# Latent attention's prologue: roots by logarithm ahead of the copies, weights of the next stage quantised inside the pair loop

## Chip, cores and metric

One core of one Trainium2 chip runs the whole kernel. The metric is the device time of one execution in microseconds (us), median over several runs.

## What is computed

The reference is a decoder of two layers over `x` with 8 rows of 128 tokens and 256 features. Each of six stages is a layer norm, an operation, and an addition to `x`: (1) a spectral attention, (2) a long convolution with the context, (3) a mixture of 8 experts of which each token takes 2, (4) latent attention, (5) cross attention with int8 weights, (6) a ternary feed-forward. The change lies in stage 4 and in the preparation of stage 5:

```python
def _layernorm(x, axis=-1, eps=1e-05):
    m = jnp.mean(x, axis=axis, keepdims=True)
    v = jnp.var(x, axis=axis, keepdims=True)
    return (x - m) / jnp.sqrt(v + eps)
...
q_latent = hidden_states @ Wqa
q = (q_latent @ Wqb).reshape(b, s, H, Q_HEAD_DIM)
kv_comp = hidden_states @ Wkva
c_kv, k_pe = (kv_comp[..., :KV_LORA], kv_comp[..., KV_LORA:])
q_pe, k_pe = _apply_rope(q_pe, cos, sin), _apply_rope(k_pe, cos, sin)
scores = jnp.einsum('bhqd,bhkd->bhqk', q_full, k_full) * scale   # 16 heads, causal
probs = jax.nn.softmax(scores, axis=-1)
out = (probs @ v) @ Wo
...
def _qdq(x):                       # stage 5, weights and activations
    s = jnp.maximum(jnp.max(jnp.abs(x), axis=-1, keepdims=True) / 127.0, 1e-08)
    return jnp.clip(jnp.round(x / s), -127.0, 127.0) * s
```

## The kernel before

Every engine has its own instruction stream, written out by hand in one block each (`sp`, `pool`, `act`, `dve`, `pe`), and the streams meet only at semaphores: `wait_ge` holds everything that stands behind it on its engine. Nothing is scheduled by a planner; the order of the source is the order on the engine. `then` on VectorE (DVE) chains an instruction to the one before it.

Stage 3 ends with 16 gathers on GpSimd (POOL, L489): four per pair of token rows, semaphore `gathered{pair}`. SyncE (SP) issues, from L411 on, the weights of stage 5 (`w5_loaded`) and the transposed context (`cxT_loaded`) as soon as the last expert product is in PSUM (`l3_psum`).

Stage 4 works on four pairs of rows. Its prologue, before the pair loop, does for each pair i: `add_experts(i)` on DVE (the expert rows are added to `x`, L1110, with the statistics, L889), then `normalise(4, ...)` (L899): variance plus eps into `ve` (`ln_var`), a root, `rsqrt_refined` (one Newton step), and `xn` (L909). The root is taken on ScalarE (ACT) by `deviation(n, lo, hi)` (L550): `sd = sqrt(ve)`, and DVE takes the reciprocal of it (L881). TensorE (PE) turns `xn` (`turn_pair(i)`, L1579), ACT copies it out of PSUM (`xnT_pair(i)`). For pair 0 alone the prologue also has PE make the latents (`latents`), eight groups of queries (`queries_low`, `queries_high`, L1623 and L1627, in two alternating PSUM banks) and the keys (`key_latents`, `turn_kv`); ACT copies each group (`queries(0, j)`, L704), POOL rotates it (`rope_q`, L499 to L503), and PE may start group j only when ACT has copied group j - 2 (`q4_copied`). Behind the last pair, DVE quantises the stage-5 weights `ew` (L1170 to L1178: largest value, scales, `ediag`, `eqf`, `eqi`), and only then gives the semaphores `s4_masked`, `pT_ready`, `x4_added` their start values.

`pair4(i, after)` is then the attention of pair i, with the queries of pair i + 1 worked in: a `Fori` of three rounds on each of PE, ACT, DVE and POOL, and a fourth call without a next pair. Its waits count with the loop register. Per round POOL rotates eight query groups and divides eight groups of probabilities (`divide`, L508). The tail of a round is the products with the values, the output projection (L1682), `rope_k(after, u)` (L1147 to L1152) and `add_tile` (L1120) on DVE.

`preload(f)` on ACT (L548) is an activation on one value whose only use is that the table of `f` is loaded then: `Sqrt` ahead of the prologue, `Exp` ahead of the pair loop, `Sqrt` behind it, `Exp` and `Sqrt` around stage 5's pair loop.

## Time and profile before

| | us |
|---|---|
| three runs | 782.61, 782.74, 784.62 (median 782.74) |
| the profiled execution | 780.92 |
| its span, first to last instruction | 778.7 |
| PE, DVE, ACT, POOL busy | 587.9, 462.9, 309.4, 261.6 |
| granted TensorE clock, mean | 0.885 of full |

The profile covers one execution, whose time is 2.2 us more than its span. All times below are microseconds from the span's start. A busy share over the whole span mixes six stages with different limits. What the change is worth has to be read in the stretch from 374, where stage 3 ends, to 437, where the first round of the pair loop has POOL busy, and at the two roots of stages 5 and 6 (near 608 and 709).

### The profile page before, as it was taken

What the parts mean: (1) busy time and instruction counts of PE and PEld (TensorE: products, weight loads), DVE (VectorE), ACT (ScalarE), POOL (GpSimd) and SP (SyncE); (2) the same over time, 40 slices, a digit from 0 to 9 for tenths busy, and PEclk for the clock granted to TensorE, in tenths of its full rate; (3) what the DMA queues carried; (4) which work ended last, traced back from release to release, by engine and by line L of the source; (5) the groups of instructions that cost most, each with busy time, mean ns of one, the idle gap of its engine ahead of it and who ended that gap; (6) DMA issues with size and microseconds to landing.
All of it is one profiled execution on the core that took longest, in us unless ns stands there. A gap on an engine that the chain in (4) does not pass through costs nothing.

```text
span 778.7 us, 12968 instructions
## 1 busy us (share of the span) xinstructions
PE 587.9 (75%) x4241; PEld 425.7 (55%) x4242; DVE 462.9 (59%) x1004; ACT 309.4 (40%) x738; POOL 261.6 (34%) x300
## 2 busy tenths in 40 slices
PE   3857896455599999999174989989888677762665
PEld 3446343334488888898032656656576265552333
DVE  3677999674455455554168352524445846868695
ACT  1511201425233333333122562736555445554463
POOL 4930688758000000000466580936713310100000
PEclk9979999556699999999776899999999999996697
DMA  7693202456311111110610000000000400000000
GB/s 271 226 388 127 86 1 70 147 182 243 109 36 45 54 54 38 43 55 29 196 49 0 0 1 1 0 0 0 0 0 1 162 1 2 2 2 1 0 27 28
DMA packets 34245, 52.11 MB, mean 67 GB/s; under 512 B 3096, under 2 KB 24160, under 8 KB 33824
## 3 DMA queue, kind: packets, MB, share of 16 engines
q1 hardware_dynamic: 31680, 43.49, 16.7%
q0 software_dynamic: 2528, 8.13, 2.8%
q8 instruction: 23, 0.38, 0.2%
q14 instruction: 14, 0.11, 0.0%
HBM read 40.60 MB, written 11.01 MB: 66 GB/s over the span
## 4 chain that ended last, share of the span: by engine, by line
PE 45%; DVE 19%; POOL 13%; issue 12%; ACT 7%; DMA 3%; SPq 0%; POOLq 0%; ACTq 0%; DVEq 0%
PE bank L1533 15%; PE bank L1546 5%; POOL rq L501 3%; POOL sm L508 3%; POOL sorted_rows L483 3%; POOL rq L499 2%; PE bank L1412 2%; PE bank L1682 2%; PE bank L1441 2%; DVE xn L909 2%; PE bank L1443 2%; PE bank L1442 2%; PE bank L1944 1%; ACT pT L803 1%; PE bank L1843 1%
## 5 line engine op out<-in xcount | busy, mean ns | idle before, releaser
L1533 PE MATMUL bank<-h,wsp 128*128 128x256 f16 x720 | 81.3, 273 | 2.0 <-DVE h L1088 1.2
L654 ACT ACTIVATE hf<-bank,be 128x256 f32<-128x256 f32 x120 | 50.4, 471 | 81.5 <-PE bank L1533 72.9
L489 POOL DMA_INDIRECT yg<-expert_rows,pos x16 | 15.7, 981 | 186.5 <-DMA expert_rows<-yb 181.9
L1533 PEld LDWEIGHTS bank<-h,wsp 128*128 x720 | 69.5, 98 | 12.1 <-issue 3.8
L1086 DVE CAST h<-hf 128x512 f16<-128x512 f32 x60 | 25.6, 427 | 65.5 <-ACT hf L654 64.0
L698 ACT ACTIVATE sm<-sm,nm 128x128 f32<-128x128 f32 x128 | 49.8, 394 | 1.0 <-DVE nm L1198 1.0
L471 POOL TENSOR_TENSOR kvp<-xnT,cxT 128x512 f32<-128x512 f32 x32 | 35.6, 1136 | 42.9 <-ACT xnT L558 33.0
L564 ACT CAST wsp<-wraw 128x2048 f16<-128x2048 f32 x12 | 22.6, 1900 | 66.1 <-DMA wraw<-in_L_ffn_W 66.1
L448 POOL TENSOR_TENSOR wsp<-wraw,wsp 128x512 f16<-128x512 f32 x40 | 45.8, 1176 | 8.5 <-ACT wsp L564 8.2
L1195 DVE SCALAR_TENSOR_TENSOR sm<-bank,const 128x512 f32<-128x512 f32 x32 | 22.1, 692 | 38.1 <-PE bank L1649 38.1
L1533 PE MATMUL bank<-xgT,wsp 128*128 128x256 f16 x360 | 43.9, 281 | 0.1
L499 POOL TENSOR_TENSOR rq<-qs,const 128x256 f32<-128x256 f32 x32 | 23.6, 737 | 59.1 <-ACT qs L704 59.1
L1546 PE MATMUL bank<-wsp,h 128*128 x360 | 41.9, 273 | 1.6 <-DVE h L1088 1.6
L1088 DVE TENSOR_TENSOR h<-hf,h 128x512 f16<-128x512 f32 x60 | 41.5, 692 | 2.1
L508 POOL TENSOR_TENSOR sm<-sm,rinv 128x512 f32<-128x512 f32 x32 | 33.1, 1040 | 26.1 <-DVE rinv L1189 26.1
L1533 PEld LDWEIGHTS bank<-xgT,wsp 128*128 x360 | 36.3, 101 | 5.6 <-issue 0.5
L1546 PEld LDWEIGHTS bank<-wsp,h 128*128 128x128 f16 x360 | 35.1, 98 | 5.9 <-issue 1.8
L1627 PE MATMUL bank<-wqb,ql 128*128 128x512 f32 x64 | 35.3, 639 | 0.0
L1649 PE MATMUL bank<-kT,qT 128*128 128x128 f32 x256 | 34.0, 276 | 0.9 <-ACT qT L711 0.9
L1218 DVE COPY pT<-bank 128x512 f32<-128x512 f32 x32 | 21.7, 682 | 18.5 <-PE bank L1660 18.0
L1660 PE MATMUL bank<-const,sm 128*128 128x128 f32 x128 | 22.0, 300 | 13.7 <-POOL sm L508 10.5
L1649 PEld LDWEIGHTS bank<-kT,qT 128*128 128x128 f32 x256 | 31.3, 192 | 1.5 <-ACT qT L711 1.3
(291 smaller groups left out, 1359.8 us busy)
## 6 DMA issues: line engine op xcount, KB each, us to landing
wraw<-in_L_ffn_W SPq DMA_DIRECT2D x16, 512.0 KB, 4.5
wraw<-in_L_ffn_W SPq DMA_DIRECT2D x8, 1024.0 KB
sorted_rows<-early POOLq DMA_DIRECT2D x2, 1920.0 KB, 14.3
xg<-sorted_rows SPq DMA_DIRECT2D x15, 256.0 KB, 2.8
expert_rows<-yb SPq DMA_DIRECT2D x15, 256.0 KB, 2.2
cxT<-in_ctxT SPq DMA_DIRECT2D x2, 1024.0 KB, 9.3
tap<-in_taps SPq DMA_DIRECT2D x1, 2048.0 KB, 14.3
x<-in_x SPq DMA_DIRECT2D x1, 1024.0 KB, 5.8
```

The source lines that it names most:

```text
L448: last = nc.gpsimd.tensor_tensor(wsp[:, e, 1, part], wraw[:, half, 512 * q:512 * q + 512], wsp[:, e, 0, part], ALU.subtract)
L471: nc.gpsimd.tensor_tensor(kvp[:, h % 2, c, :].rearrange("p (b i j) -> p b i j", b=NT, i=CH), xnT[:, c, :, g].unsqueeze(3).to_broadcast([P, ...
L499: nc.gpsimd.tensor_tensor(rq[:, g % 2, 0], v, cosb, ALU.mult).then_inc(sem("rope_step"), 1)
L508: nc.gpsimd.tensor_tensor(sm[:, u, hs, :], sm[:, u, hs, :], rinv[:, u, hs].unsqueeze(2).to_broadcast([P, 4, P]), ALU.mult).then_inc(sem("p ...
L654: last = nc.scalar.activation(hf[:, p, SLOTS * k:SLOTS * k + SLOTS], bank[2 * (layer - 1) + p][:, SLOTS * k:SLOTS * k + SLOTS], ACT.Gelu, ...
L698: last = nc.scalar.activation(sm[:, u, h, :], sm[:, u, h, :], ACT.Exp, bias=nm[:, u, h:h + 1], accum_out=rsum[:, u, h:h + 1])
L1086: nc.vector.tensor_copy(hi, hf[:, p, :]).then_inc(sem("h_hi"), 1)
L1088: nc.vector.tensor_tensor(h[:, 1, 2 * p:2 * p + 2, :].rearrange("p f n -> p (f n)"), hf[:, p, :], hi, ALU.subtract).then_inc(sem(f"h{layer ...
L1533: last = nc.tensor.matmul(b[:, SLOTS * (f % 2):SLOTS * (f % 2) + SLOTS], w[a_][:, c, P * f:P * f + P], inp[:, b_, c, :], start=(c == 0 and ...
L1546: last = nc.tensor.matmul(bank[4 + u][:, D * b:D * b + D], h2[:, b_, c, P * b:P * b + P], w[a_][:, c, :], start=(c == 0 and a_ + b_ == 0), ...
L1627: nc.tensor.matmul(four_heads(bank[1 + k][:]), ql0[:, u, :], wqb[:, k, :, a_:a_ + 4, :].rearrange("p w h n -> p h w n"), start=False, stop ...
L1649: last = nc.tensor.matmul(bank[5 + g % 2][:, P * k:P * k + P], qT[:, u, 4 * g + k, :], kT[:, u, :], start=True, stop=True)
```

## The change

In words, engine by engine:

- SP waits, ahead of the stage-5 loads, for the last of the gathers.
- `deviation(n, ...)` with n of 4 or more (the four of the prologue, and those of stages 5 and 6) writes ln(ve) into `sd`, waits for itself, and writes exp(-0.5 sd) into `rs`; DVE no longer takes the reciprocal. All `preload(ACT.Exp)` and `preload(ACT.Sqrt)` from the prologue on are gone, and the first is `preload(ACT.Ln)`.
- On ACT and PE the roots and the turns of pairs 1 to 3 stand further ahead between the copies and products of the queries. On DVE `rope_k(0, 0)` and `rope_k(0, 1)` stand behind the norms of pairs 2 and 3.
- The quantisation of `ew` is cut in three parts, and part i stands in the tail of pair i, ahead of its `rope_k`. The semaphores get their start values ahead of the prologue.
- The pair loop is written out on all four engines.

```diff
             sp.wait_ge(sem("l3_psum"), ET)
+            sp.wait_ge(sem(f"gathered{NT // 2 - 1}"), 16 * 4)
...
                 act.wait_ge(sem("ln_var"), n)
-                nc.scalar.activation(sd[:, lo:hi], ve[:, lo:hi], ACT.Sqrt).then_inc(sem("ln_sd"), 1)
+                if n < 4:
+                    nc.scalar.activation(sd[:, lo:hi], ve[:, lo:hi], ACT.Sqrt).then_inc(sem("ln_sd"), 1)
+                else:
+                    nc.scalar.activation(sd[:, lo:hi], ve[:, lo:hi], ACT.Ln).then_inc(sem("ln_log"), 1)
+                    act.wait_ge(sem("ln_log"), n - 3)
+                    nc.scalar.activation(rs[:].rearrange("p t k -> p k t")[:, 0, lo:hi], sd[:, lo:hi], ACT.Exp, scale=-0.5).then_inc(sem("ln_sd"), 1)
...
-            preload(ACT.Sqrt)
+            preload(ACT.Ln)
...
             deviation(4, 0, 2)
             xnT_pair(0)
+            deviation(5, 2, 4)
...
             query_latents(0)
+            xnT_pair(1)
             queries(0, 0)
             key_latents(0, 0)
-            deviation(5, 2, 4)
-            for j in range(1, 4):
-                queries(0, j)
-            xnT_pair(1)
+            deviation(6, 4, 6)
+            queries(0, 1)
+            queries(0, 2)
+            xnT_pair(2)
+            deviation(7, 6, 8)
+            queries(0, 3)
             queries(0, 4)
             key_latents(0, 1)
-            deviation(6, 4, 6)
             queries(0, 5)
-            xnT_pair(2)
-            deviation(7, 6, 8)
+            xnT_pair(3)
             queries(0, 6)
             queries(0, 7)
-            xnT_pair(3)
-            preload(ACT.Exp)
-            with act.Fori(0, NT // 2 - 1) as i:
-                pair4(i, i + 1)
-            pair4(NT // 2 - 1, None)
-
-            preload(ACT.Sqrt)
+            for i in range(NT // 2):
+                pair4(i, i + 1 if i + 1 < NT // 2 else None)
+
             deviation(8)
...
             magnitudes(0)
-            preload(ACT.Exp)
...
-            preload(ACT.Sqrt)
             outputs5(NT - 1)
...
-                then(nc.vector.reciprocal(r[:, 0], root))
+                if root is not None:
+                    then(nc.vector.reciprocal(r[:, 0], root))
...
-            for i in range(2):
-                add_experts(i)
-                normalise(4, 4 + i, 2 * i, 2 * i + 2)
-            rope_k(0, 0)
-            add_experts(2)
-            normalise(4, 6, 4, 6)
-            rope_k(0, 1)
-            add_experts(3)
-            normalise(4, 7, 6, 8)
...
             dve.sem_inc(sem("s4_masked"), 2)
             dve.sem_inc(sem("pT_ready"), 2)
             dve.sem_inc(sem("x4_added"), 1)
+            for i in range(NT // 2):
+                add_experts(i)
+                normalise(4, 4 + i, 2 * i, 2 * i + 2)
+                if i >= 2:
+                    rope_k(0, i - 2)
...
                     for t in range(NT - 2):
                         stats(5, t)
+                quantise_weights(i)
                 for u in range(2):
                     if after is not None:
                         rope_k(after, u)
...
             latents(0)
+            turn_pair(1)
             queries_low(0, 0)
...
             queries_high(0, 2)
+            turn_pair(2)
             queries_high(0, 3)
-            turn_pair(1)
             queries_low(0, 4)
             queries_high(0, 4)
             pe.wait_ge(sem("kvr_ready"), 1)
             key_latents(0, 1)
             queries_high(0, 5)
-            turn_pair(2)
+            turn_pair(3)
             turn_kv(0, 1)
             queries_low(0, 6)
             queries_high(0, 6)
             queries_high(0, 7)
-            turn_pair(3)
             pe.wait_ge(sem("xnT_act"), 10)
-            with pe.Fori(0, NT // 2 - 1) as i:
-                pair4(i, i + 1)
-            pair4(NT // 2 - 1, None)
+            for i in range(NT // 2):
+                pair4(i, i + 1 if i + 1 < NT // 2 else None)
```

The order on ScalarE before, from the root of pair 0 on (`sd` is the root, `xnT` the turned pair, `ql` the query latents, `qs` a query group, `kvT` the key latents; the names in brackets are semaphores):

```order
L553 ACTIVATE sd<-ve 128x2 [waits ln_var]
L679 COPY xnT<-bank 128x2x256 [waits xnT_psum]
L688 COPY ql<-bank 128x256 [waits lat_psum]
L689 COPY ql<-bank 128x256
L704 COPY qs<-bank 128x512 [waits q4_psum]
L693 COPY kvT<-bank 128x128 [waits kv_psum]
L553 ACTIVATE sd<-ve 128x2 [waits ln_var]
L704 COPY qs<-bank 128x512 [waits q4_psum] x3
L679 COPY xnT<-bank 128x2x256 [waits xnT_psum]
```

The same place in the changed kernel (`rs` is the inverse root; its line numbers are some lines higher):

```order
L556 ACTIVATE sd<-ve 128x2 [waits ln_var]
L558 ACT_TABLE_LOAD
L558 ACTIVATE rs<-sd 128x2 [waits ln_log]
L684 COPY xnT<-bank 128x2x256 [waits xnT_psum]
L556 ACT_TABLE_LOAD
L556 ACTIVATE sd<-ve 128x2 [waits ln_var]
L558 ACT_TABLE_LOAD
L558 ACTIVATE rs<-sd 128x2 [waits ln_log]
L694 COPY ql<-bank 128x256 [waits lat_psum]
L695 COPY ql<-bank 128x256
L684 COPY xnT<-bank 128x2x256 [waits xnT_psum]
L710 COPY qs<-bank 128x512 [waits q4_psum]
```

The root of pair 1 moved from behind the first query group to ahead of the latents, and every root is now a logarithm and an exponential with a table load ahead of each.

Further on, ScalarE before, from the second query group of pair 0 to the last root:

```order
L704 COPY qs<-bank 128x512 [waits q4_psum] x3
L679 COPY xnT<-bank 128x2x256 [waits xnT_psum]
L704 COPY qs<-bank 128x512 [waits q4_psum]
L693 COPY kvT<-bank 128x128 [waits kv_psum]
L553 ACTIVATE sd<-ve 128x2 [waits ln_var]
L704 COPY qs<-bank 128x512 [waits q4_psum]
L679 COPY xnT<-bank 128x2x256 [waits xnT_psum]
L553 ACTIVATE sd<-ve 128x2 [waits ln_var]
```

And in the changed kernel, from the root of pair 2 on:

```order
L556 ACTIVATE sd<-ve 128x2 [waits ln_var]
L558 ACT_TABLE_LOAD
L558 ACTIVATE rs<-sd 128x2 [waits ln_log]
L710 COPY qs<-bank 128x512 [waits q4_psum] x2
L684 COPY xnT<-bank 128x2x256 [waits xnT_psum]
L556 ACT_TABLE_LOAD
L556 ACTIVATE sd<-ve 128x2 [waits ln_var]
L558 ACT_TABLE_LOAD
L558 ACTIVATE rs<-sd 128x2 [waits ln_log]
L710 COPY qs<-bank 128x512 [waits q4_psum] x2
L699 COPY kvT<-bank 128x128 [waits kv_psum]
```

The last root, which waits for the variance of pair 3, moved from behind six query groups to behind three.

VectorE before, at the end of the prologue (`esc` scales, `ediag`, `eqf`, `eqi` the quantised weights; `sm` the scores of the first round):

```order
L909 TENSOR_SCALAR xn<-x,mv,rs 128x256
L1171 TENSOR_REDUCE esc<-ew 128x4 [waits w5_loaded]
L1166 TENSOR_SCALAR esc<-esc 128x4 [waits dve_own]
L1167 RECIPROCAL esc<-esc 128x4 [waits dve_own]
L1176 TENSOR_SCALAR eqf<-ew,esc 128x256 [waits dve_own] x2
L1175 TENSOR_SCALAR ediag<-const,esc 128x128 [waits dve_own]
L1176 TENSOR_SCALAR eqf<-ew,esc 128x256 [waits dve_own]
L1175 TENSOR_SCALAR ediag<-const,esc 128x128 [waits dve_own]
L1176 TENSOR_SCALAR eqf<-ew,esc 128x256 [waits dve_own]
```

VectorE in the changed kernel, in the tail of the first round (`pT` turned probabilities, `kvr` and `rk` the keys of the next pair, `x` with `bank` the added output):

```order
L1222 COPY pT<-bank 128x512 [waits pt4_psum]
L1192 RECIPROCAL rinv<-rsum 128x4 [waits exp_ready] x2
L1222 COPY pT<-bank 128x512 [waits pt4_psum] x3
L1175 TENSOR_REDUCE esc<-ew 128x4 [waits w5_loaded]
L1167 TENSOR_SCALAR esc<-esc 128x4 [waits dve_own]
L1168 RECIPROCAL esc<-esc 128x4 [waits dve_own]
L1149 COPY kvr<-bank 128x64 [waits kvn_psum,dve_own]
L1150 TENSOR_TENSOR rk<-bank,const 128x64
L1152 TENSOR_TENSOR rk<-bank,const 128x32 x2
L1154 TENSOR_TENSOR kvr<-rk 128x64 [waits rk_step]
L1122 TENSOR_TENSOR x<-x,bank 128x256 [waits out4_psum]
```

The first part of the quantisation moved out of the stretch between the last norm and the first round, to between the last copy of probabilities and the key rotation of a round's tail.

## Rows read from the trace of the kernel before

**Rows 1.** The page: busy time, share of the span, instructions of an engine.

```profile
PE 587.9 (75%) x4241; PEld 425.7 (55%) x4242; DVE 462.9 (59%) x1004; ACT 309.4 (40%) x738; POOL 261.6 (34%) x300
```

**Rows 2.** The chain that ended last, 374 to 440: start, duration, what.

```profile
380.70 6.68 DMA yg<-expert_rows,pos
...
424.78 12.68 issue
```

**Rows 3.** The gathered tile `yg`: issue to landing.

```profile
DMA to landing us min/median/max: 2.7/3.0/7.4
```

**Rows 4.** VectorE in order of time, 374 to 440: start, duration, instruction, idle before.

```profile
387.40 1.01 DVE L1110 SCALAR_TENSOR_TENSOR x<-yg,top,x 128x256 f32<-128x256 f32 x2 [16.16 <-DMA yg<-expert_rows,pos]
...
390.49 0.17 DVE L904 TENSOR_SCALAR ve<-mv 128x2 f32<-128x2 f32 x1
...
391.13 0.16 DVE L882 TENSOR_TENSOR nw<-rs 128x2 f32<-128x2 f32 x1
...
402.34 0.17 DVE L881 RECIPROCAL rs<-sd 128x2 f32<-128x2 f32 x1 [6.37 <-ACT sd L553]
...
406.33 1.34 DVE L1110 SCALAR_TENSOR_TENSOR x<-yg,top,x 128x256 f32<-128x256 f32 x2
...
409.90 0.49 DVE L904 TENSOR_SCALAR ve<-mv 128x2 f32<-128x2 f32 x1
...
422.99 1.21 DVE L1171 TENSOR_REDUCE esc<-ew 128x4 f32<-128x1024 f32 x1
...
424.87 1.07 DVE L1176 TENSOR_SCALAR eqf<-ew,esc 128x256 f32<-128x256 f32 x2
...
427.39 0.69 DVE L1177 TENSOR_SCALAR eqf<-eqf 128x1024 f32<-128x1024 f32 x1
```

**Rows 5.** Source lines of table loads and roots: shortest, median, longest, in ns.

```profile
L548 ACT ACT_TABLE_LOAD  x7: 1283/1283/1283, 196.0 to 715.0; - x7
...
L553 ACT ACTIVATE sd<-ve x9: 203/208/217, 10.1 to 709.3; 128x8 f32<-128x8 f32 x5, 128x2 f32<-128x2 f32 x4
```

**Rows 6.** TensorE in order of time, 374 to 440, and 462 to 496.

```profile
394.71 3.78 PE L1592 MATMUL bank<-xnT,wqa 128*128 128x256 f32 x8 [0.68 <-ACT xnT L679]
...
407.11 1.13 PE L1623 MATMUL bank<-wqb,ql 64*128 64x512 f32 x4 [0.24 <-ACT qs L704]
...
409.58 1.02 PE L1627 MATMUL bank<-wqb,ql 128*128 128x512 f32 x2
...
414.98 2.08 PE L1623 MATMUL bank<-wqb,ql 64*128 64x512 f32 x4
...
428.41 1.09 PE L1641 MATMUL bank<-const,qs 128*128 128x128 f32 x4 [4.17 <-DVEq L1180]
...
477.36 0.60 PE L1641 MATMUL bank<-const,qs 128*128 128x128 f32 x4
```

**Rows 7.** A stretch: busy time of PE, PEld, DVE, ACT, POOL; granted clock, DMA share, GB/s.

```profile
413.00:419.00 6.00, 5.27 (x12) 2.40 (x13) 4.41 (x12) 0.59 (x1) 4.83 (x8) 0.50 0.00 0
```

**Rows 8.** GpSimd in order of time: its first rotation of rounds 0 and 1.

```profile
437.49 0.73 POOL L499 TENSOR_TENSOR rq<-qs,const 128x256 f32<-128x256 f32 x1 [12.09 <-ACT qs L704]
...
484.70 0.73 POOL L499 TENSOR_TENSOR rq<-qs,const 128x256 f32<-128x256 f32 x1 [19.72 <-ACT qs L704]
```

**Rows 9.** VectorE in the tail of round 0.

```profile
467.50 0.21 DVE L1147 COPY kvr<-bank 128x64 f32<-128x64 f32 x1
...
470.82 0.42 DVE L1120 TENSOR_TENSOR x<-x,bank 128x256 f32 x1 [2.51 <-PE bank L1682]
```

**Rows 10.** VectorE and ScalarE at the roots of stages 5 and 6.

```profile
608.43 0.20 DVE L881 RECIPROCAL rs<-sd 128x8 f32<-128x8 f32 x1 [0.28 <-ACT sd L553]
...
709.43 3.74 ACT L832 COPY fguT<-bank 128x1024 bf16<-128x1024 bf16 x4
...
717.81 1.23 DVE L1236 TENSOR_SCALAR xn<-xn 128x2048 f32<-128x2048 f32 x1 [0.22 <-ACT xn L839]
```

**Rows 11.** DMA queues, 605 to 700: packets, MB, share of 16 engines.

```profile
q8 instruction: 8, 0.13, 0.6%
```

More of the change, by code:

```diff
@@ L523, in _ @@
                 rope_q(0, j // 4, j % 4)
-            with pool.Fori(0, NT // 2 - 1) as i:
-                pair4(i, i + 1)
-            pair4(NT // 2 - 1, None)
+            for i in range(NT // 2):
+                pair4(i, i + 1 if i + 1 < NT // 2 else None)
             pool.wait_ge(sem("x4_added"), NT + 1)
@@ L906, in normalise @@
                 r2 = rs[:].rearrange("p t k -> p k t")
-                rsqrt_refined(ve[:, lo:hi], sd[:, lo:hi], r2[:, :, lo:hi], nw[:, :, lo:hi])
+                rsqrt_refined(ve[:, lo:hi], sd[:, lo:hi] if n < 4 else None, r2[:, :, lo:hi], nw[:, :, lo:hi])
                 for t in range(lo, hi):
@@ L1152, in rope_k @@
                 nc.vector.tensor_tensor(kvr[:, u, 64:128], rk[:, 0], rk[:, 1], ALU.add).then_inc(sem("kvr_ready"), 1)
-            for i in range(2):
+            dve.sem_inc(sem("s4_masked"), 2)
+            dve.sem_inc(sem("pT_ready"), 2)
+            dve.sem_inc(sem("x4_added"), 1)
+            for i in range(NT // 2):
                 add_experts(i)
                 normalise(4, 4 + i, 2 * i, 2 * i + 2)
-            rope_k(0, 0)
-            add_experts(2)
-            normalise(4, 6, 4, 6)
-            rope_k(0, 1)
-            add_experts(3)
-            normalise(4, 7, 6, 8)
+                if i >= 2:
+                    rope_k(0, i - 2)
             def scales(dst_scale, dst_inverse, largest, floor):
@@ L1167, in scales, with quantise_weights @@
                 then(nc.vector.reciprocal(dst_inverse, dst_scale))
-            dve.wait_ge(sem("w5_loaded"), 112)
-            ew4 = ew[:].rearrange("p w c n -> p (w c) n")
-            then(nc.vector.tensor_reduce(esc[:, 0, :], ew4, AX.X, ALU.max, apply_absolute_value=True))
-            scales(esc[:, 1, :], esc[:, 2, :], esc[:, 0, :], True)
-            for k in range(4):
-                if k >= DC:
-                    then(nc.vector.tensor_scalar(ediag[:, k - DC, :], cst["ident"], esc[:, 1, k:k + 1], None, ALU.mult))
-                then(nc.vector.tensor_scalar(eqf[:, k, :], ew4[:, k, :], esc[:, 2, k:k + 1], ROUND, ALU.mult, ALU.add))
-            then(nc.vector.tensor_scalar(eqf[:], eqf[:], -ROUND, 127.0, ALU.add, ALU.min))
-            nc.vector.tensor_scalar(eqi[:], eqf[:], -127.0, None, ALU.max).then_inc(sem("eqi_ready"), 1)
-            dve.sem_inc(sem("s4_masked"), 2)
-            dve.sem_inc(sem("pT_ready"), 2)
-            dve.sem_inc(sem("x4_added"), 1)
+            def quantise_weights(part):
+                ew4 = ew[:].rearrange("p w c n -> p (w c) n")
+                if part == 0:
+                    dve.wait_ge(sem("w5_loaded"), 112)
+                    then(nc.vector.tensor_reduce(esc[:, 0, :], ew4, AX.X, ALU.max, apply_absolute_value=True))
+                    scales(esc[:, 1, :], esc[:, 2, :], esc[:, 0, :], True)
+                elif part == 1:
+                    for k in range(4):
+                        if k >= DC:
+                            then(nc.vector.tensor_scalar(ediag[:, k - DC, :], cst["ident"], esc[:, 1, k:k + 1], None, ALU.mult))
+                        then(nc.vector.tensor_scalar(eqf[:, k, :], ew4[:, k, :], esc[:, 2, k:k + 1], ROUND, ALU.mult, ALU.add))
+                elif part == 2:
+                    then(nc.vector.tensor_scalar(eqf[:], eqf[:], -ROUND, 127.0, ALU.add, ALU.min))
+                    nc.vector.tensor_scalar(eqi[:], eqf[:], -127.0, None, ALU.max).then_inc(sem("eqi_ready"), 1)
             causal = cst["causal"].unsqueeze(1).to_broadcast([P, 4, P])
@@ L1218, in copy_pT @@
                 nc.vector.tensor_copy(pT[:, u, 4 * g:4 * g + 4, :].rearrange("p h n -> p (h n)"), bank[3 + g % 2][:]).then_inc(sem("pT_ready"), 1)
-            with dve.Fori(0, NT // 2 - 1) as i:
-                pair4(i, i + 1)
-            pair4(NT // 2 - 1, None)
+            for i in range(NT // 2):
+                pair4(i, i + 1 if i + 1 < NT // 2 else None)
             nc.vector.tensor_tensor(bkm[:], bk5[:].unsqueeze(2).to_broadcast([P, DC, 2]), cst["parity"].unsqueeze(1).to_broadcast([P, DC, 2]), ALU.mult).then_inc(sem("bkm_ready"), 1)
@@ L1750, in _ @@
             queries_high(0, 7)
-            turn_pair(3)
             pe.wait_ge(sem("xnT_act"), 10)
-            with pe.Fori(0, NT // 2 - 1) as i:
-                pair4(i, i + 1)
-            pair4(NT // 2 - 1, None)
+            for i in range(NT // 2):
+                pair4(i, i + 1 if i + 1 < NT // 2 else None)
             x_done(pe, 4, NT - 1)
```

## Prediction

> **What bounds the kernel now.** I read the page first, then the chain that ended last, then each engine in order of time in the stretch that the change touches. The page says little here: TensorE is busy for 75% of the span [rows 1], but that is an average over six stages. The chain of 374 to 440 says more. The reader is to see two things in it: 6.68 us of waiting for a gather at its head, and 12.68 us from 424.78 on, in which no work of the chain runs before the pair loop has GpSimd going [rows 2]. From there a round is set by GpSimd and the tail behind it: its first rotation starts at 437.49 in round 0 and at 484.70 in round 1, 47.2 us apart [rows 8]. So all that the prologue gains shifts the time of that first rotation, and I ask when it starts after the change.
>
> The prologue before has three stalls. VectorE gets its first rows at 387.40 [rows 4], although a gather lands in 3.0 us as a rule and this one took 6.68 [rows 2, 3]: the stage-5 weights were in the queues. It then waits 6.37 us for the root of pair 1, because that root stands behind a query group on ScalarE [rows 4]. And it quantises weights from 422.99 on, while TensorE waits 4.17 us for the start values behind that work, to 428.41 [rows 4, 6].
>
> **The change, step by step** (new times on the clock of the trace before).
>
> *Gathers first.* The fourth gather is issued at 380.70; with 3.0 us it lands at 383.7, 3.7 earlier. Between 2.7 and the old 6.68 us the gain is 4.0 to 0; the first is near, since the cause of the long one is moved away. The loads behind it are needed one whole round later and stay hidden; if they came late, quantising would hold the tail of round 0.
>
> *Roots by logarithm.* A root cost 0.21 us of ScalarE and a reciprocal. It is now Ln 0.21, a table load 1.28 and Exp 0.21 in a row, since the order shows a load ahead of each of the two; the load ahead of Ln can run while the variance is awaited [rows 5]. From the variance's end at 390.66 to the Newton step at 391.13 it was 0.47 us [rows 4]; it becomes 1.75: +1.28 for each root on the path.
>
> *The chain on VectorE.* A pair's additions and statistics take 3.26 us (387.40 to 390.66) or, beside GpSimd's rotations, 4.06 (406.33 to 410.39) [rows 4]. Newton step and norm take 1.7 us for a pair, to 2.9 beside GpSimd, read from 391.13 and 402.34 on to the next additions, at most 3.1 and 4.0 with the key rotation in them. So: additions from 383.7, variance 0 at 386.9, its root at 388.7, norm 390.4. Pair 1: variance 393.6, root 395.3 (it was 402.34), norm 397.0. Pair 2: variance 400.3.
>
> *ScalarE and TensorE beside it.* TensorE turns pair 0 at 390.4 and has the latents (3.78 us) at 396.0 [rows 6]. Now it must turn pair 1 first, at 397.0 to 398, and the first query group is copied near 400.3, about 1.2 earlier than before. ScalarE copies it and the keys, and at 400.9 turns to root 2: load 1.28, Ln 0.21, load 1.28, Exp 0.21, together 3.0 us, to 403.9. Only then does it copy group 1, and TensorE can start group 2 at 404.5; here the change is some 1.1 us **behind** the kernel before. VectorE has norm 2 at 406.6, the keys at 407.5, and pair 3's variance at 411.4.
>
> *The new wait.* On ScalarE root 3 stands ahead of the copy of group 3. Its Ln waits for the variance at 411.4, and load and Exp take it to 413.1. Behind it stand the copies of groups 3 to 7, and TensorE waits for group 3's copy before group 4: it starts that at 413.7, where it was 407.11 [rows 6]. So ordering the roots ahead gives VectorE back its 6.37 us and takes 6.6 from the queries. But all four norms are then done at about 416, and nothing but query work is left.
>
> *To the first round.* From group 4 to the end of group 5 TensorE needed 3.49 us (407.11 to 410.60) at the full clock [rows 6]. The turns of pair 3 and of the keys, a wait for a copy, and groups 6 and 7, which take what 4 and 5 take, add 3.7: 7.2 in all. But TensorE has stood for some 5 us before 413.7. Before the change the clock was at 0.50, its lower level of 1.2 GHz, from 413 to 419, after TensorE had stood from 410.60, although it was busy 5.27 of those 6 us [rows 7]; the same two products took 2.08 instead of 1.13 us [rows 6]. I add 2.3 us for some 5 us at the lower clock: round 0 begins at 423.2 instead of 428.41, **-5.2**. In exchange the round begins with the clock up. From a round's first product to GpSimd's first rotation it was 9.08 us in round 0 (428.41 to 437.49) and 7.34 in round 1 (477.36 to 484.70) [rows 6, 8]: **-1.7**. First rotation at 430.5: **-6.9**. With the full clock throughout it is -9.3 (413.7 + 7.2 + 7.34 = 428.2); with the lower clock all through, 413.7 + 13 + 9.1 = 435.8, -1.7.
>
> *Quantising in the tails.* Part 0 takes 1.88 us (422.99 to 424.87), part 1 2.52 (to 427.39), part 2 1.4 [rows 4]. The room: in the tail of round 0 VectorE has its copies done at 467.5, rotates keys for 0.8 us, and then waits 2.51 us for the output product, to 470.82 [rows 9]. Parts 0 and 2 fit; part 1 ends its keys at 467.5 + 2.5 + 0.8 = 470.8: **+0.1**. Were there no room, it would be 5.8 in three tails.
>
> *Written-out loop.* The first product of round 1 follows at 477.36 with no idle time noted ahead of it [rows 6], so the way back cost nothing there: **0**. What it can cost is below.
>
> *Stages 5 and 6.* The Exp table that the removed preloads brought is there from root 8 on; both preloads stood in waits of ScalarE and give nothing. Root 8 is on the path: VectorE waits only for it at 608.43 [rows 10], so it pays 1.28 more: **+1.3**. After root 9 ScalarE copies six blocks from 709.43 on, and VectorE at 717.81 waits for ScalarE by 0.22 [rows 10]; ScalarE is later by a load and an Exp, 1.28 + 0.21: **+1.5**.
>
> Sum: -6.9 + 0.1 + 1.3 + 1.5 = **-4.0 us**. The profiled execution took 780.92, 1.8 below the median of 782.74; from the median, 778.7.
>
> **A rule against the rows.** The trace shows table loads of 1.283 us and no gap that it charges to them [rows 5], and the order shows Ln and Exp each with its own load. The Trainium skill (ScalarE: Activation LUTs, "What ACT_TABLE_LOAD costs") gives the same 1283 ns, but adds a drain of about 1380 ns to each switch of sets; by its figure each of the places above would cost twice as much, and the result would be near no change. The same page ("Table sets: the hidden batching unit") has one set that holds both Ln and Exp, with one load for the pair. The built program doesn't use it, by the order's rows.
>
> **Rivals.**
> - *A switch costs twice its load.* Four places on the path (roots 0, 3, 8, 9) would each cost another load's time, if the engine had to empty around it: 4 x 1.28 = 5.1, and 782.74 - 4.0 + 5.1 = 783.8, no change. Against it: the root in rows 10 is answered within 0.28 us, and nothing idle is charged to loads. 8%.
> - *The clock stays low through the prologue*, since TensorE now has two rests (near 402 and 409): -1.7 + 2.9 is +1.2, 783.9; half way from the forecast, 781.3. For it: rows 7; against it: the long busy run from 413.7. 12%, within 0.3% mostly.
> - *Slower: code.* Three more copies of a round on four engines must be fetched. If each new page stalled TensorE for a transfer of some 2.7 us [rows 3] in the tails, where TensorE is the path, five stalls are +13.5: 792. From two stalls (5.4) on it eats the gain, and three give 786.8. Against it: 8 such fetches lie in 605 to 700, in straight code [rows 11]. 9%.
> - *More is won.* The clock stays up (-9.3), or the loop's register work was on the path: 776.3. 14%. The Trainium skill (Runtime: NRT & Kernel Launch, "Instruction fetch mechanics") holds that a taken branch outside the fetched pages stalls; by it writing out gains, but the trace shows no stall at 477.36.
> - *The loads are not there* (one table for both): roots 0, 3, 8, 9 without 1.28, 773.6. The order speaks against it. 2%.
> - *My forecast*, 776.8 to 780.8: 55%.
>
> **Numbers.** A measurement of this kernel tells about 0.3%, 2.35 us, from no change. Faster by that is below 780.4: nearly all of the forecast's 55, the 14 and 2, in all 0.69. Within: 0.20. Slower: 0.11. The range, 775.0 to 782.8, leaves out the code rival, the full drain and the shared table, and holds the bounds of the clock in part.
>
> **What the next profile would show.** First additions on VectorE near 383.7; its wait for root 1 at 1.7 us, not 6.4; 16 table loads instead of 9; ScalarE idle ahead of the Ln of root 3, and a TensorE gap of some 5 us ending near 413.7; first round near 423; first rotation near 430.5, each round then 47.2; Newton steps of stages 5 and 6 later by 1.3 against what is ahead of them. The prediction fails if ScalarE's root 3 is released much earlier or later than 413, if the clock doesn't return before the first round, or if the rounds' period changes.

## The result, and the profile after

The changed kernel takes 776.86 us (median of four runs, 776.02 to 778.14), the kernel before in the same comparison 783.19: ratio 0.9921, 95% interval 0.990 to 0.9942. A second series gave 772.87 against 782.41, 0.9897 (0.986 to 0.9934). So it is faster by 6 to 10 us. The forecast, 778.7, had the sign and the mechanism; the gain of 4.0 was too small.

From the page of the profiled execution, which took 776.70 us where that of before took 780.92 (the row that answers to [rows 1] is the second):

```profile
span 774.9 us, 12670 instructions
PE 590.2 (76%) x4241; PEld 425.4 (55%) x4242; DVE 459.4 (59%) x998; ACT 319.3 (41%) x747; POOL 257.2 (33%) x300
```

ScalarE has 9.9 us more to do and the kernel is faster. What the busy time buys is in the order. The first gather is issued at 379.13, against 376.89 before: stages 1 to 3, which the change leaves alone, took 2.2 us longer in this execution. All times of after below carry these 2.24 us against the clock of before.

The gathered tile, and VectorE in order of time:

```profile
DMA to landing us min/median/max: 2.7/2.7/2.8
```

```profile
385.69 1.00 DVE L1112 SCALAR_TENSOR_TENSOR x<-yg,top,x 128x256 f32<-128x256 f32 x2 [12.10 <-DMA yg<-expert_rows,pos]
...
395.35 0.17 DVE L906 TENSOR_SCALAR ve<-mv 128x2 f32<-128x2 f32 x1
...
397.31 0.16 DVE L884 TENSOR_TENSOR nw<-rs 128x2 f32<-128x2 f32 x1 [1.78 <-issue]
...
401.91 0.17 DVE L906 TENSOR_SCALAR ve<-mv 128x2 f32<-128x2 f32 x1
...
405.66 0.16 DVE L884 TENSOR_TENSOR nw<-rs 128x2 f32<-128x2 f32 x1 [3.58 <-ACT rs L558]
...
412.75 0.17 DVE L906 TENSOR_SCALAR ve<-mv 128x2 f32<-128x2 f32 x1
```

The long landing of [rows 3] is gone, and the wait for the root of pair 1 fell from 6.37 [rows 4] to 1.78. What replaced it is on ScalarE, around the roots of pairs 2 and 3:

```profile
402.62 1.28 ACT L556 ACT_TABLE_LOAD   x1
403.91 0.20 ACT L556 ACTIVATE sd<-ve 128x2 f32<-128x2 f32 x1
404.13 1.28 ACT L558 ACT_TABLE_LOAD   x1
405.43 0.20 ACT L558 ACTIVATE rs<-sd 128x2 f32<-128x2 f32 x1
405.54 0.57 ACT L710 COPY qs<-bank 128x512 f32<-128x512 f32 x1
...
412.95 0.20 ACT L556 ACTIVATE sd<-ve 128x2 f32<-128x2 f32 x1 [2.19 <-DVE ve L906]
413.17 1.28 ACT L558 ACT_TABLE_LOAD   x1
414.47 0.20 ACT L558 ACTIVATE rs<-sd 128x2 f32<-128x2 f32 x1
414.58 0.57 ACT L710 COPY qs<-bank 128x512 f32<-128x512 f32 x1
```

A root for two values a lane now holds ScalarE for 2.9 us (402.62 to 405.54), and the next copy of queries starts 1.63 us after the variance of pair 3 releases ScalarE (412.95 to 414.58). TensorE, and then GpSimd:

```profile
406.16 1.13 PE L1626 MATMUL bank<-wqb,ql 64*128 64x512 f32 x4 [3.00 <-ACT qs L710]
...
415.20 2.08 PE L1626 MATMUL bank<-wqb,ql 64*128 64x512 f32 x4 [5.56 <-ACT qs L710]
...
423.90 0.60 PE L1644 MATMUL bank<-const,qs 128*128 128x128 f32 x4
```

```profile
431.21 0.73 POOL L500 TENSOR_TENSOR rq<-qs,const 128x256 f32<-128x256 f32 x1 [1.69 <-ACT qs L710]
...
476.78 0.73 POOL L500 TENSOR_TENSOR rq<-qs,const 128x256 f32<-128x256 f32 x1 [18.05 <-ACT qs L710]
```

Two new waits, 3.00 and 5.56 us, and no wait at the first round any more (4.17 in [rows 6]). The clock in the same stretch (columns as in [rows 7]):

```profile
415.00:418.00 3.00, 2.80 (x5) 1.00 (x6) 1.98 (x5) 0.14 (x1) 2.44 (x4) 0.50 0.03 5
418.00:421.00 3.00, 2.90 (x13) 1.58 (x11) 0.07 (x1) 1.37 (x4) 1.26 (x3) 0.89 0.00 0
421.00:424.00 3.00, 2.98 (x9) 1.21 (x10) 1.26 (x5) 1.05 (x2) 2.84 (x6) 1.00 0.00 0
```

After the rest of 5.56 us TensorE works at 0.50, its level of 1.2 GHz, and is back at full by the third row, before the first round. At the roots of stages 5 and 6, where [rows 10] is before, VectorE shows:

```profile
601.76 0.17 DVE L884 TENSOR_TENSOR nw<-rs 128x8 f32<-128x8 f32 x1 [1.80 <-ACT rs L558]
```

```profile
707.16 0.17 DVE L884 TENSOR_TENSOR nw<-rs 128x8 f32<-128x8 f32 x1 [1.80 <-ACT rs L558]
...
715.41 1.23 DVE L1239 TENSOR_SCALAR xn<-xn 128x2048 f32<-128x2048 f32 x1 [0.46 <-ACT xn L840]
```

### The profile page after: what moved, and what is told of

The parts are those of the page before. It is cut to its first block, busy times and chain, and to the rows that moved or that the text cites. A ratio compares the mean times of both kernels' runs of the same rounds, so it can differ in the third digit from the quotient of the medians.

```text
span 774.9 us, 12670 instructions
## 1 busy us (share of the span) xinstructions
PE 590.2 (76%) x4241; PEld 425.4 (55%) x4242; DVE 459.4 (59%) x998; ACT 319.3 (41%) x747; POOL 257.2 (33%) x300
## 4 chain that ended last, share of the span: by engine, by line
PE 52%; DVE 16%; POOL 12%; ACT 11%; issue 4%; DMA 3%; another core or an unknown queue 0%; SPq 0%; ACTq 0%; DVEq 0%
PE bank L1536 16%; PE bank L1549 5%; PE bank L1685 4%; POOL sm L509 3%; POOL rq L502 3%; POOL qs L504 2%; POOL rq L500 2%; PE bank L1415 2%; ACT pT L805 2%; PE bank L1444 2%; PE bank L1446 2%; PE bank L1445 2%; DMA wraw<-in_L_ffn_W 1%; PE bank L1845 1%; PE bank L1946 1%
## 5 line engine op out<-in xcount | busy, mean ns | idle before, releaser
L1685 PE MATMUL bank<-wo4a,oT 128*128 128x256 f32 x128 | 32.5, 404 | 0.0
L502 POOL TENSOR_TENSOR rq<-qs,const 128x128 f32<-128x128 f32 x64 | 31.9, 520 | 0.0
```

The costliest lines, as they stand in the source:

```text
L502: nc.gpsimd.tensor_tensor(turned[:, :, :, two], pairs[:, :, :, 1 - two], sinb[:, :, :, two], ALU.mult).then_inc(sem("rope_step"), 1)
L1685: last = nc.tensor.matmul(bank[7][:, 0:D], oT[:, u, j, :], wvo[:, j, :], start=(j == 0), stop=(j == H4 // 2 - 1))
```

## Experiments

To compare profiled executions I cut each into stretches between marks that every variant has. The columns: from the first gather to the first product of round 0; from there to GpSimd's first rotation; round 0 from rotation to rotation; from GpSimd's memset of stage 5 to the first Newton product of its root; from there to the variance of stage 6; from that to the first clip of VectorE (L1236 before). Values are differences of two starts, in us; the last two columns are the timed runs. The runs were taken in several series, and each ratio is to the kernel before as timed in the same series (its medians were 781.6 to 783.6), so ratios and not medians are compared across rows. A trace is of one execution: in e_wait_alone, e_start_alone, e_rolled, e_sqrt, e_shared and after_again of the shortest one timed, in e_order3 of one of the longer ones.

| kernel | to round 0 | to rotation | round 0 | root 5 | stage 5 | root 6 | median | ratio |
|---|---|---|---|---|---|---|---|---|
| before | 51.52 | 9.08 | 47.21 | 4.05 | 100.44 | 8.70 | 783.19 | 1 |
| after | 44.77 | 7.31 | 45.57 | 5.33 | 103.43 | 10.22 | 776.86 | 0.9921 |
| after_again | 44.69 | 7.30 | 45.54 | 5.33 | 101.68 | 10.22 | 772.87 | 0.9897 |
| e_wait_alone | 49.24 | 8.57 | 48.65 | 4.04 | 100.77 | 8.70 | 778.73 | 0.9956 |
| e_no_wait | 51.42 | 7.30 | 45.53 | 5.33 | 101.30 | 10.22 | 782.02 | 0.9987 |
| e_start_alone | 48.19 | 8.98 | 47.17 | 4.06 | 100.07 | 8.70 | 779.76 | 0.9972 |
| e_quant_prologue | 46.90 | 7.31 | 45.55 | 5.33 | 103.42 | 10.22 | 778.28 | 0.9938 |
| e_rolled | 44.62 | 7.40 | 45.70 | 5.34 | 104.65 | 10.22 | 778.32 | 0.9968 |
| e_sqrt | 40.20 | 8.78 | 47.22 | 4.05 | 100.90 | 8.70 | 768.84 | 0.9831 |
| e_shared | 39.15 | 7.30 | 45.57 | 4.05 | 103.39 | 8.94 | 774.73 | 0.9898 |
| shared_again | 42.29 | 7.31 | 46.99 | 4.05 | 104.67 | 8.94 | 772.95 | 0.9866 |
| e_order3 | 45.58 | 7.31 | 46.77 | 5.33 | 103.30 | 10.22 | 776.18 | 0.9934 |
| e_order3_sqrt | 35.42 | 7.95 | 47.03 | 4.05 | 100.86 | 8.70 | 765.17 | 0.9806 |
| e_order3_shared | 35.56 | 7.31 | 47.10 | 4.05 | 101.72 | 8.95 | 760.57 | 0.9728 |

The ratios' 95% intervals reach 0.002 to 0.004 to either side. Only e_order3_shared is beyond 2% with its whole interval.

**The gathers' wait, alone and taken out.** On the kernel before:

```diff
             sp.wait_ge(sem("l3_psum"), ET)
+            sp.wait_ge(sem(f"gathered{NT // 2 - 1}"), 16 * 4)
```

> The kernel before with one line of the change: SyncE waits for the last gather ahead of the stage-5 loads. My account: the first additions start 3.7 to 4.0 us earlier and everything behind them in the prologue shifts: 779.3 us, 3.9 less than before. Rival, the roots behind the query copies take it back: 783.

And the same line taken out of the changed kernel:

> The changed kernel without the wait for the last gather. My account: the first additions are 3.7 to 4.0 us later, the whole prologue with them: 780.7 us. Rival, root 3 stands on ScalarE and is bound by the table loads, not by the first gather: 777.

Alone the wait gives 0.44% (interval of the ratio 0.9931 to 0.9981), some 3.4 us. Without it the changed kernel is no faster than before: 782.02, ratio 0.9987 (0.9963 to 1.0011). Its gathers then land, in the view of the tile and on VectorE:

```profile
388.66 1.01 DVE L1111 SCALAR_TENSOR_TENSOR x<-yg,top,x 128x256 f32<-128x256 f32 x2 [17.85 <-DMA yg<-expert_rows,pos]
```

```profile
DMA to landing us min/median/max: 2.7/4.1/8.4
```

The wait for the first rows, 12.10 us in the changed kernel, is 17.85 here: the line is worth 5.75 us of VectorE's start in this execution, where the fourth gather of before landed 3.7 later than the usual 3.0. Taken out of the change it costs 0.66 to 0.90% by the two ratios of the changed kernel, the largest effect of a part tried, and without it the rest is within 0.3%. That the rest is worth nothing doesn't follow: in this trace the first additions come 12.19 us after the first gather's issue, 1.7 later than before (10.51), and TensorE has the low clock at group 0 (2.08 us for its first products), both of which are in its 51.42 us to round 0.

**The start values alone.** On the kernel before, the three increments of VectorE moved ahead of the prologue:

```diff
+            dve.sem_inc(sem("s4_masked"), 2)
+            dve.sem_inc(sem("pT_ready"), 2)
+            dve.sem_inc(sem("x4_added"), 1)
             for i in range(2):
                 add_experts(i)
...
-            dve.sem_inc(sem("s4_masked"), 2)
-            dve.sem_inc(sem("pT_ready"), 2)
-            dve.sem_inc(sem("x4_added"), 1)
```

> The kernel before with one edit: the three start values (s4_masked, pT_ready, x4_added) are given ahead of the prologue instead of behind the quantisation. My theory: the wait of 4.17 us of TensorE at the first round's start goes, so round 0 begins some 3.5 us earlier than 428.41 on the clock of before. But VectorE is still quantising until about 428, and masks and sums of the first round stand behind that, so the first rotation on GpSimd comes earlier by less: I expect 0 to 3 us, 781 to 783 where the kernel before has 783. Rival: the start values alone carry the prologue's gain, then 8 us are won and this is 775.

779.76, ratio 0.9972 (0.9951 to 0.9993), and round 0 begins 3.3 us earlier, as expected. My bound on what that is worth was too careful. VectorE in that kernel:

```profile
426.25 0.69 DVE L1181 TENSOR_SCALAR eqi<-eqf 128x1024 bf16<-128x1024 f32 x1
429.54 0.69 DVE L1195 SCALAR_TENSOR_TENSOR sm<-bank,const 128x512 f32<-128x512 f32 x1 [2.59 <-PE bank L1649]
```

Quantising ends at 426.94 and VectorE then waits 2.59 us for the first scores. The time to rotation is unchanged (8.98), so the 3.3 us reach the first rotation in full. The timed runs have 0.28% of it, some 2.2 us, with an interval from 0.5 to 3.8.

**Quantising in one piece behind the prologue,** in the changed kernel, with the start values left early:

```diff
+            for part in range(3):
+                quantise_weights(part)
...
-                quantise_weights(i)
```

> The changed kernel with the whole quantisation back in one piece, but behind the last key rotation of the prologue, with the start values given early as changed. My account: what gained was that the start values no longer stand behind it, and VectorE has about 6 us free there (from 422.3 to the first scores at 428.4) for its 5.8 us: nothing lost, 777 us. Rival, it must be in parts in the tails: 780 or more.

778.28 (0.9938, interval 0.9909 to 0.9968), within the spread of the changed kernel. The rotation comes 7.31 us after round 0 begins, as in it, and the next stretches agree to 0.05. That round 0 begins 2.1 us later in its trace is for the most part the clock, well ahead of the quantising. Group 0 of the queries, in it and in the changed kernel:

```profile
399.51 2.08 PE L1628 MATMUL bank<-wqb,ql 64*128 64x512 f32 x4
```

```profile
399.56 1.13 PE L1626 MATMUL bank<-wqb,ql 64*128 64x512 f32 x4
```

With the two products behind them (1.93 us and 1.12) that is 1.8 us. So the early start values do the work; cutting the quantisation in three gives nothing that these rows show.

**The loop rolled again** on TensorE, ScalarE and GpSimd (VectorE's stays written out):

> The changed kernel with the pair loop a loop again on TensorE, ScalarE and GpSimd (VectorE's stays written out, since the parts of the quantisation differ by round). My account: the written-out loop gives nothing, rounds are 45.5 to 47.3 us apart in either form, by the clock: 777 us, within noise of the changed kernel. Rival, the 1.6 us that round 0 lost came from writing it out: rounds of 47.2 each and 780.

Round 0 takes 45.70 and round 1 47.22, against 45.57 and 47.09. In 425 to 590, most of the four rounds, the changed kernel has more instruction fetches than the kernel before. The DMA queues, after first, then before:

```profile
q8 instruction: 7, 0.11, 0.3%
```

```profile
q8 instruction: 2, 0.03, 0.1%
```

Neither the branches of the one nor the fetches of the other are on the path in these rows. (The Trainium skill, Runtime: NRT & Kernel Launch, "Instruction fetch mechanics", warns of a stall at a taken branch outside the fetched pages; no such stall is in these rounds.) The medians, 0.9968 against 0.9921 and 0.9897, leave 3.7 to 5.6 us, and its trace, of the shortest execution, has nothing of it in the rounds. The twelve executions fall into two groups: six of 775.6 to 777.0 with a mean clock of 0.885 to 0.889, and six of 779.7 to 782.2 with 0.877 to 0.881. The upper clocks give the times of the changed kernel in the first series (776.0 to 777.0 at 0.885 to 0.887), so what differs is how many executions had the lower one, here half, there one of four (778.1 at 0.880). Whether the loop has a part in that isn't shown.

**Square roots in the new order.** The changed kernel with `Sqrt`, the reciprocal and the preloads of before:

```diff
...
-                    nc.scalar.activation(sd[:, lo:hi], ve[:, lo:hi], ACT.Ln).then_inc(sem("ln_log"), 1)
-                    act.wait_ge(sem("ln_log"), n - 3)
-                    nc.scalar.activation(rs[:].rearrange("p t k -> p k t")[:, 0, lo:hi], sd[:, lo:hi], ACT.Exp, scale=-0.5).then_inc(sem("ln_sd"), 1)
+                    nc.scalar.activation(sd[:, lo:hi], ve[:, lo:hi], ACT.Sqrt).then_inc(sem("ln_sd"), 1)
...
```

> The changed kernel with the roots of before (square root, reciprocal on VectorE, and the preloads of Sqrt and Exp put back), all else as changed: the new order alone, without the logarithm. My account: a root costs 0.47 us again, so nearly the same as with the shared set, but the Exp preload (1.5 us) stands between the last query copy and the first round: 767 us. If the logarithm itself is what gained, this gives the gain back, 780 or more.

768.84, ratio 0.9831 (0.9797 to 0.9864): the logarithm costs the change 0.66 to 0.90%, 5 to 7 us. In the stretches: 4.6 us to round 0, 1.28 at the root of stage 5, 1.52 at that of stage 6, less 1.5 to the first rotation, where the preload of `Exp` returns (417.35). The traces differ in two more stretches, round 0 (1.65 us longer) and stage 5 (2.5 shorter), for which these roots give no cause. TensorE ahead of group 4 still waits:

```profile
406.90 2.08 PE L1625 MATMUL bank<-wqb,ql 64*128 64x512 f32 x4 [4.08 <-ACT qs L705]
```

By these rows 4.08 of the 5.56 us belong to root 3's place ahead of the copy, and 1.5 to the load and the exponential.

**The set that holds both functions.** One line:

```diff
-            preload(ACT.Ln)
+            nc.scalar.preload_act_table_set("natural_log_exp_and_others")
```

> The changed kernel with one table set that holds logarithm and exponential loaded once at 680 in place of the Ln preload: 5 table loads in all instead of 16, the arithmetic the same functions. My account (each load that stands in a root is waited for, and ScalarE's loads are what holds the query copies): every Newton step follows its variance by 0.5 us instead of 1.95, root 2 is ready 3 us earlier beside that, group 4 of the queries starts some 7 us earlier, TensorE's gap and low clock ahead of it go: about -8 in the prologue and -2.6 at the roots of stages 5 and 6, 766 us. Rival, only the four loads on the old path count: -5.1, 772. Rival, a switch also drains the engine, which the records don't show: a further -1.3 for each of the switches taken away, 761 or less. Rival, the loads are hidden: 777.

> The changed kernel with the shared table set once more, for the open question why one execution took 766.6 and the other six 772.7 to 777.7. If those six had lost time to the granted clock of that stretch of executions, most executions should now lie at 765 to 768 with a mean clock of 0.89, a ratio of 0.978 to 0.983. If the variant itself has a second course, 772 to 777 comes again, ratio near 0.99, and the loads' worth in this order is then 0 to 3 us and not 8.

The loads between logarithm and exponential go, the Newton step follows the variance by 0.5 us, and roots 5 and 6 lose 1.28 us each. The step of stage 5 in e_shared:

```profile
589.04 0.17 DVE L884 TENSOR_TENSOR nw<-rs 128x8 f32<-128x8 f32 x1 [0.52 <-ACT rs L558]
```

The time didn't follow: 774.73, then 772.95, where I expected 766. Only the profiled execution of the first took 766.62, at a mean clock of 0.890; its other six had 0.876 to 0.880. In the second series the mean clock was 0.874 to 0.888 and the times 768.5 to 777.5, and its trace shows where such an execution loses. TensorE at group 4, in e_shared and in shared_again:

```profile
405.34 1.57 PE L1626 MATMUL bank<-wqb,ql 64*128 64x512 f32 x4 [4.33 <-ACT qs L710]
```

```profile
410.74 2.08 PE L1626 MATMUL bank<-wqb,ql 64*128 64x512 f32 x4 [4.33 <-ACT qs L710]
```

The same rest of 4.33 us, and then 0.5 us more for the same products; from group 4 to round 0 it is 8.68 us (405.34 to 414.02) in the one and 10.11 (410.74 to 420.85) in the other. Stages 1 to 3, round 0 and stage 5 each add 1 to 4 us. Neither of my two readings held cleanly: the longer executions are those at the lower clock, and this variant as a rule has it; why isn't shown. With the rest at group 4 left in, removing 11 loads gives between nothing and 0.55% by these four ratios.

**Root 3 behind the copies of groups 3, 4 and the keys,** with the turn of pair 3 behind the last queries:

```diff
             xnT_pair(2)
-            deviation(7, 6, 8)
             queries(0, 3)
             queries(0, 4)
             key_latents(0, 1)
+            deviation(7, 6, 8)
             queries(0, 5)
-            xnT_pair(3)
             queries(0, 6)
             queries(0, 7)
+            xnT_pair(3)
...
-            turn_pair(3)
             turn_kv(0, 1)
             queries_low(0, 6)
             queries_high(0, 6)
             queries_high(0, 7)
+            turn_pair(3)
```

> The changed kernel with one thing moved: the last root (pair 3) stands behind the copies of query groups 3 and 4 and the keys on ScalarE, and the turn of pair 3 behind group 7 on TensorE. My account says that the 5.6 us that TensorE waits for the copy of group 3 come from the root ahead of it: group 4 starts 5 us earlier, then group 5's copy waits for the root, and round 0 begins about 4 us earlier: 773 us, and from the gather's start to round 0 41 us instead of 44.8. Rival, the wait only moves to group 5's copy and nothing is gained: 777.

> The same reordering on the kernel with the roots of before (square root and reciprocal) and the changed order otherwise. My account: no table load stands in the prologue, and root 3 comes when its variance is ready, so round 0 begins 36 us after the first gather, 4 us before the kernel with the roots of before: 765 us. This would be the fastest so far.

> The changed kernel with root 3 behind the copies of groups 3, 4 and the keys, and with one preload of the table set that holds both functions, so 5 table loads instead of 16. My theory: a root no longer blocks ScalarE for 3 us between two query copies, so the reordering now pays as it did with square roots: round 0 begins some 35 to 37 us after the first gather, and the root of stage 5 is answered in 0.5 us; 765 to 768. Rival: something other than the loads makes the logarithm's variants slow (the changed kernel with the shared set was 766.6 in one execution and 773 to 778 in the others), then this is 772 or more.

With logarithms as the change has them nothing is won: 776.18, ratio 0.9934. The 5.56 us at group 4 are gone, and the wait stands at group 6:

```profile
410.78 1.13 PE L1626 MATMUL bank<-wqb,ql 64*128 64x512 f32 x4 [0.68 <-ACT qs L710]
...
417.32 1.13 PE L1626 MATMUL bank<-wqb,ql 64*128 64x512 f32 x4 [2.94 <-ACT qs L710]
```

since ScalarE still takes two loads in a row between two copies:

```profile
413.78 1.28 ACT L556 ACT_TABLE_LOAD   x1
415.07 0.20 ACT L556 ACTIVATE sd<-ve 128x2 f32<-128x2 f32 x1
415.29 1.28 ACT L558 ACT_TABLE_LOAD   x1
```

Its trace is of an execution at the lower clock (0.877, 778.4 us; those at 0.885 and more took 773.0 to 776.3), and it met the low clock earlier, at groups 0 and 1: 2.08 and 1.76 us for products that took 1.13 and 1.12 in the changed kernel. Less these 1.6 us the prologue would be 44.0 (an estimate), 0.8 below the changed kernel's. Take the loads away, and the same move shortens the prologue by 4.8 us with square roots (40.20 to 35.42) and by 3.6 to 6.7 with the shared set (39.15 and 42.29 to 35.56). The medians follow clearly for the set, 760.57 (0.9728, interval 0.9692 to 0.9765), 22 us under the kernel before and the fastest of all; with square roots, 765.17 (0.9806, interval 0.9772 to 0.9841), the interval still meets that of the order as it was. In that last kernel ScalarE has the root of pair 3 between two copies, and TensorE no rest above 0.73 us from the first query group to round 0:

```profile
404.94 0.22 ACT L556 ACTIVATE sd<-ve 128x2 f32<-128x2 f32 x1
405.19 0.20 ACT L558 ACTIVATE rs<-sd 128x2 f32<-128x2 f32 x1
405.61 0.59 ACT L710 COPY qs<-bank 128x512 f32<-128x512 f32 x1 [0.21 <-PE bank L1630]
```

```profile
402.08 1.13 PE L1626 MATMUL bank<-wqb,ql 64*128 64x512 f32 x4 [0.68 <-ACT qs L710]
...
406.25 1.13 PE L1626 MATMUL bank<-wqb,ql 64*128 64x512 f32 x4 [0.57 <-ACT qs L710]
```

```profile
402.00:408.00 6.00, 5.35 (x19) 2.32 (x20) 5.04 (x14) 1.68 (x6) 5.84 (x10) 1.00 0.77 253
```

The clock is at 1.00 in these six us. From e_order3 to this kernel the prologue loses 10.0 us (1.4 of them at groups 0 and 1, where the clock was low in e_order3), the roots of stages 5 and 6 2.6, and stage 5 1.6.

**The changed kernel again:**

> The changed kernel unchanged, on the same chip and beside the same runs of the kernel before as the two above: 776 to 778, ratio 0.991 to 0.994. If it is off by more, the comparisons across the groups of runs are less sure than their intervals say.

The ratio, 0.9897, is outside the expected 0.991 to 0.994 and just below the first interval (0.990 to 0.9942), though the two intervals overlap; the median, 772.87, is 3 us under the expected 776 to 778. By what I had written down, comparisons across the series are less sure than their intervals say: two ratios of one kernel differ by 0.0024. The differences of e_quant_prologue and e_start_alone are of that size; those of e_sqrt against the changed kernel, of the two order3 variants without loads against e_order3, and of the gathers' wait are larger. Its stretches up to the rounds agree with the first trace to 0.1 us. Stage 5 differs, by 1.75 us, with nothing changed.

## Why the prediction was right, and where it was off

Times of after less 2.24, against the forecast's own clock. The median of the first series, 776.86, lies in the forecast's range; the second series' ratio would make 774.7 of 782.74, just below the range's lower end of 775.0.

- *Gathers first.* First additions at 383.45 (forecast 383.7). Right, also in that the loads behind them are needed much later.
- *Roots by logarithm.* VectorE waits 1.78 us between the end of a variance and the Newton step (1.75 forecast), and the steps start at 388.48 and 395.07 (forecast 388.7 and 395.3). At stages 5 and 6 the costs are 1.28 and 1.52, forecast 1.3 and 1.5. The rival in which a switch costs twice its load is out: each load starts within 0.03 us of the end before it and the next activation within 0.03 of its own end. The Trainium skill's figure of some 1380 ns of drain for a switch (ScalarE: Activation LUTs, "What ACT_TABLE_LOAD costs") doesn't show in any row here. The same page ("Table sets: the hidden batching unit") is right that one set holds both functions, and e_shared and e_order3_shared used it, with 5 loads; the program as built has 16, with one ahead of each `Ln` and each `Exp` of these roots.
- *The new wait.* Predicted as 5 us or so ending at 413.7, it was 5.56 us ending at 412.96. Group 2, forecast 404.5, started at 403.92.
- *To the first round: the term that was mis-sized.* "From group 4 on 7.2 us, and 2.3 for some 5 us at the lower clock" gives 9.5; it took 8.70. The rows of the clock have it low from 415.2 to near 418.7; group 4's products took 2.08 and 1.84 us there, and 1.13 and 1.12 at group 2, which is 1.7 us in all. With group 4 itself 0.7 earlier than forecast, from a prologue of VectorE that ran a little shorter, the first rotation moved by -8.5 (60.60 to 52.08) and not by -6.9. The 7.34 us to the first rotation was 7.31. The clock was back before the first round, which answers the rival in which it stays low.
- *Quantising and the written-out loop* at nothing: the quantising holds in the rows, the loop in the rounds' rows, and the medians of e_rolled go by its clock. The rival in which fetches cost five stalls has nothing in these rows.
- *Not in the forecast: the clock elsewhere.* The forecast had each round at 47.2 us and named a changed period of the rounds as a sign of being wrong. Round 1 is 47.09, but round 0 is 45.57, 1.64 us shorter, although TensorE meets the same wait for GpSimd's last division in its tail, 2.76 us before and 2.77 after:

```profile
464.04 1.12 PE L1660 MATMUL bank<-const,sm 128*128 128x128 f32 x4 [2.76 <-POOL sm L508]
```

```profile
457.79 0.66 PE L1663 MATMUL bank<-const,sm 128*128 128x128 f32 x4 [2.77 <-POOL sm L509]
```

  The clock around it, in the kernel before and then after:

```profile
461.00:467.00 6.00, 3.24 (x17) 3.00 (x16) 1.55 (x4) 2.25 (x9) 3.90 (x6) 0.74 0.00 0
```

```profile
455.00:461.00 6.00, 3.23 (x22) 2.91 (x22) 2.96 (x5) 1.97 (x7) 3.66 (x6) 1.00 0.00 0
```

  It isn't an accident of one trace: round 0 takes 45.5 to 45.7 us in six of the nine traces with logarithms and 46.8 to 47.1 in three, and 47.0 to 48.7 in the five with square roots. Why the clock falls behind this rest in the one and not in the other isn't shown. In stage 5 it went the other way: 3.0 us longer in the one trace of after and 1.2 in the other. The kernel before and the four variants with square roots have 100.1 to 100.9 there, the nine with logarithms 101.3 to 104.7. The two groups don't overlap; were it chance alone, five given traces of fourteen would be the five lowest once in 2002 times. So something in the variants with logarithms most likely costs time there, for which the forecast has nothing. The clock goes with the larger part: it is 0.82 to 0.85 in the six traces of 103.3 to 104.7, and 0.88 to 0.89 in the three of 101.3 to 101.7, as with square roots (0.87 to 0.90). What lowers it, and what the remaining half a microsecond or more is, isn't shown.

The sum of the profiled pair: +2.24 -8.52 -1.64 -0.27 (later rounds) +1.28 +2.99 +1.52 -1.40 (behind the last clip) = -3.8 of span; the executions differ by 4.2, 780.92 to 776.70, since the part outside the span is 1.8 us and not 2.2. That this is near the forecast's -4.0 is partly luck, since terms that the change doesn't own are in it. The prologue and the two roots, the parts that it owns, make -5.7, and the medians -6.3 and -9.5.

What the forecast missed is what the change throws away. It named the wait of root 3 and priced it, but took it as given, and it knew of a shared set only as one that the program doesn't load. With cheap roots and root 3 three copies further back the whole is worth 1.94% (square roots) or 2.72% (shared set), 15 or 21 us. The logarithm with its two loads gives back 5 to 7 of these in the order as it stands, and 10 or 16 in the better one (ratios 0.9934 against 0.9806 and 0.9728). Part of these differences is clock, as the stretches of stage 5 and round 0 show, and isn't separated from the loads.

## What to carry to other kernels

An activation on a critical chain costs its engine the table loads around it, and the copies queued behind it pay as well as the one who waits for the result; check which table set the built program loads, not which set could serve. Before moving a waiting instruction ahead, list what stands behind it and who is released by that: the same root moved three copies back was worth at most a microsecond with loads ahead of it and 4 to 7 us of the prologue without. And a bulk load that is needed a stage later should not share queues with a gather that opens the next stage: one wait was worth 0.44% alone and 0.66 to 0.90% within this change. And when executions of one kernel come at two clocks, look at which of them the trace is from before reading a small difference out of it.

## What the runs showed of the hardware

- The same rest of TensorE doesn't always lower its clock, or not for as long. After 2.8 us of rest it was 0.74 over six us in one trace and 1.00 in the other; after 4.33 us the first products took 1.57 us or 2.08.
- Stretches without any edit vary with it: stages 1 to 3, to the first gather, took from 374.8 to 379.1 us over the fourteen traces, and runs of one kernel spread over 4 to 11 us where five or more were timed, the longer ones as a rule at the lower mean clock (in e_rolled 775.6 to 777.0 at 0.885 to 0.889, 779.7 to 782.2 at 0.877 to 0.881).
- A table load of 1.28 us is the whole price of a switch here; ScalarE showed no gap above 0.03 us around it.
- Loads issued beside gathers hold them up. A gather of the changed kernel lands in 2.7 to 2.8 us; with the stage-5 loads issued ahead it was up to 7.4 us in the kernel before and 8.4 in e_no_wait.
- Root 3 ahead of the copy of group 3 holds TensorE for at least 4 us whatever the function is (4.08 with `Sqrt`, 4.33 with the shared set, 5.56 with two loads): the most of it is the variance, which is late, and not the root.
